# Fetching the last tile's rows of the last gather by single-row DMAs from SyncE and ScalarE instead of GpSimd

## The reference, cut to what matters

```python
x = x + 0.5 * ffn(layernorm(x))
x = x + attention(layernorm(x))
x = x + 0.5 * ffn(layernorm(x))

# ffn: t = rmsnorm(x) * scale; 32 experts, the best 4 for each token
vals, idx = top_k(t @ gate_w.T + gate_b, 4)
w = softmax(vals)
combine[token, idx] += w
h = swiglu(einsum('th,efh->tef', t, w1) + b1)          # for the chosen experts alone in the kernel
out = einsum('tef,ehf->th', h * combine, w2) + combine @ b2
result = t_in + out
```

## Time and profile before

| | |
|---|---|
| median of three runs | 724.93 us |
| the profiled execution's span | 722.9 us |
| TensorE busy | 531.0 us (73%) |
| GpSimd busy | 506.2 us (70%) |
| VectorE busy | 436.2 us (60%) |
| ScalarE busy | 347.2 us (48%) |
| GpSimd's 256 gathers (L564) | 245.0 us busy, 957 ns each |
| DMA, mean over the span | 150 GB/s |

### The profile page before, as it was taken

How to read it: one execution, slowest core, us unless ns; L and a number is a source line. 1 busy time by engine, 2 the same in 40 slices (tenths; PEclk the granted TensorE clock), 3 DMA queues, 4 the chain that set the end, 5 groups by cost and what they waited for, 6 DMA issues and landing times. The chain is left out here.

```text
span 722.9 us, 12843 instructions
## 1 busy us (share of the span) xinstructions
PE 531.0 (73%) x3252; PEld 443.8 (61%) x3253; DVE 436.2 (60%) x1243; ACT 347.2 (48%) x752; POOL 506.2 (70%) x551
## 2 busy tenths in 40 slices
PE   6258879999899999385607854999999999933000
PEld 3154366999899998253504553699998999833000
DVE  6889233555547778378993868255564767845222
ACT  4444413666556666495606644366665666610000
POOL 3677777777527777777677777777752777767765
PEclk9556999999999999797557955999999999977555
DMA  7997115566546664222111111456655666524222
GB/s 271 392 375 289 52 54 153 197 194 200 175 147 197 199 210 154 81 54 53 48 52 54 51 52 55 138 182 208 203 168 177 201 198 206 160 78 128 66 62 58
DMA packets 56493, 108.28 MB, mean 150 GB/s; under 512 B 12576, under 2 KB 19968, under 8 KB 56320
## 3 DMA queue, kind: packets, MB, share of 16 engines
q1 hardware_dynamic: 40064, 74.13, 30.7%
q0 software_dynamic: 16384, 33.59, 16.1%
HBM read 51.00 MB, written 56.62 MB: 149 GB/s over the span
## 5 line engine op out<-in xcount | busy, mean ns | idle before, releaser
L564 POOL DMA_INDIRECT YG<-ys,row x256 | 245.0, 957 | 116.9 <-issue 75.4
L539 POOL DMA_INDIRECT xs<-U,row x256 | 250.7, 979 | 81.9 <-issue 74.6
L1311 PE MATMUL PS<-W,xT 128*128 x768 | 182.2, 380 | 0.2
L1311 PEld LDWEIGHTS PS<-W,xT 128*128 128x128 f32 x768 | 138.4, 190 | 16.1 <-issue 1.2
L1005 DVE TENSOR_SCALAR glulin<-PS 128x512 f32<-128x512 f32 x96 | 66.3, 691 | 127.8 <-PE PS L1320 84.3
L626 ACT ACTIVATE yrow<-PS 128x512 f32<-128x512 f32 x96 | 57.3, 597 | 103.3 <-PE PS L1320 103.3
L1320 PEld LDWEIGHTS PS<-W,hidT 128*128 128x128 f32 x768 | 100.7, 193 | 7.8 <-issue 3.4
L1320 PE MATMUL PS<-W,hidT 128*128 x768 | 102.8, 277 | 1.6 <-issue 1.2
L1018 DVE SCALAR_TENSOR_TENSOR hid<-glulin,swish 128x512 f32<-128x512 f32 x96 | 66.6, 694 | 16.0 <-ACT swish L631 10.5
L631 ACT ACTIVATE swish<-glulin 128x512 f32<-128x512 f32 x96 | 60.4, 629 | 30.5 <-DVE glulin L1005 26.7
L639 ACT ACTIVATE xT<-PS 128x512 f32<-128x512 f32 x96 | 56.3, 589 | 38.8 <-PE PS L1214 38.7
(11 more groups left out here) (178 smaller groups left out, 714.2 us busy)
## 6 DMA issues: line engine op xcount, KB each, us to landing
xrow<-xs SPq DMA_DIRECT2D x96, 256.0 KB
ys<-yrow SPq DMA_DIRECT2D x96, 256.0 KB
xs<-YG SPq DMA_DIRECT2D x6, 2048.0 KB, 13.7
W<-in_w12T SPq DMA_DIRECT2D x1, 6144.0 KB, 33.5
xs<-U,row POOLq DMA_INDIRECT x256
YG<-ys,row POOLq DMA_INDIRECT x256, 2.5
out<-X SPq DMA_DIRECT2D x7, 256.0 KB, 2.6
X<-in_x SPq DMA_DIRECT2D x4, 256.0 KB, 3.6
```

The lines of the kernel that those rows point to most:

```text
L539: pool.indirect_dma_start(out=xs[c], out_offset=bass.IndirectOffsetOnAxis(ap=row[:, i:i + 1], axis=0), in_=U[:, (c * CT + t) * H:(c * CT + ...
L564: pool.indirect_dma_start(out=YG[:, t * TOPK + k, :], out_offset=None, in_=ys[c], in_offset=bass.IndirectOffsetOnAxis(ap=row[:, i:i + 1], ...
L1311: last = te.matmul(h1, xT[:, r, q * P:(q + 1) * P], W[:, bass.ds(es[q], 2 * H)], start=True, stop=True)
```

## The change

Tile 15 of phase 3 is left out of GpSimd's gather, which ends with tile 14. Its 128 rows x 4 choices are fetched by a new function, `gather_rows`: for each partition p the four slots are loaded from `row` into registers of the issuing engine, and four DMAs of one row (512 bytes) each are issued, with the register in their source address. SyncE fetches partitions 0 to 63, 32 of them ahead of the four stores of chunk 0 and 32 ahead of those of chunk 1; ScalarE fetches partitions 64 to 127 behind its last copies. Both wait first until all of yrow is stored and phase 2 is added (`combined` at 192), since tile 15's place in YG is still read until then.

On VectorE the last two tiles change places: tile 15 is added first, after `sync_gathered` and `act_gathered` have counted all 512 DMAs, and tile 14 last, its last addition behind `last_gathered`. SyncE's stores at the end are tiles 12 and 13, tile 15, and tile 14.

```diff
+SYNC_ROWS = 64
...
+        def gather_rows(eng, first, stop, done):
+
+            t, c = CT - 1, NCHUNK - 1
+            for p in range(first, stop):
+                i = c * PAIRS + t * TOPK
+                _, at = nc.values_load_multi_w_load_instructions(
+                    row[p:p + 1, i:i + TOPK], engines=[eng.engine], min_val=0, max_val=SLOTS - 1,
+                    skip_runtime_bounds_check_because="the ranks and the tiles' begins keep them below SLOTS")
+                for k in range(TOPK):
+                    eng.dma_start(YG[p:p + 1, t * TOPK + k, :], ys[c][bass.ds(at[k], 1), :]).then_inc(done, 16)
...
@@ sync
+            for r in range(2):
+                sp.wait_ge(yrow_stored[r], 16 * (NG // 2) * NPHASE)
+            sp.wait_ge(combined, PAIRS * (NPHASE - 2) + TOPK * CT)
             for c in range(NCHUNK):
+                gather_rows(sp, SYNC_ROWS // 2 * c, SYNC_ROWS // 2 * (c + 1), sync_gathered)
                 for g in range(NCG):
...
-                    n = CG - 1 if t + CG == NTILE else CG
+                    n = CG - 2 if t + CG == NTILE else CG
...
-            sp.wait_ge(combined, PAIRS * NPHASE)
-            sp.dma_start(out_v[NTILE // CG - 1][:, CG - 1], X[:, (NTILE - 1) * H:NTILE * H]).then_inc(out_stored, 16)
+            for n in (CG - 1, CG - 2):
+                if n == CG - 2:
+                    sp.wait_ge(combined, PAIRS * NPHASE)
+                t = NTILE - CG + n
+                sp.dma_start(out_v[NTILE // CG - 1][:, n], X[:, t * H:(t + 1) * H]).then_inc(out_stored, 16)
@@ gpsimd, gather(ph)
-                for t in range(CT):
+                last = CT - 2 if ph == NPHASE - 1 else CT - 1
+                for t in range(last + 1):
...
-                        ).then_inc(last_gathered if ph == NPHASE - 1 and (t, k) == (CT - 1, TOPK - 1)
+                        ).then_inc(last_gathered if ph == NPHASE - 1 and (t, k) == (last, TOPK - 1)
@@ scalar
             experts(1)
             add_b2(1)
+            for r in range(2):
+                act.wait_ge(yrow_stored[r], 16 * (NG // 2) * NPHASE)
+            act.wait_ge(combined, PAIRS * (NPHASE - 2) + TOPK * CT)
+            gather_rows(act, SYNC_ROWS, P, act_gathered)
@@ vector, combine(ph, first, stop)
-                    pairs[-1:] = [(stop - 2,), (stop - 1,)]
+                    pairs[-1:] = [(stop - 1,), (stop - 2,)]
...
+                    if ph == NPHASE - 1 and t0 == CT - 1:
+                        dve.wait_ge(sync_gathered, 16 * TOPK * SYNC_ROWS)
+                        dve.wait_ge(act_gathered, 16 * TOPK * (P - SYNC_ROWS))
+                    else:
+                        for t in tiles:
+                            dve.wait_ge(gathered[t % 2], 16 * (TOPK * ((ph * CT + t) // 2 + 1) - ending))
```

More of the change, by code:

```diff
@@ L267, in build @@
         last_gathered = sem("last_gathered")
+        sync_gathered = sem("sync_gathered")
+        act_gathered = sem("act_gathered")
         combined = sem("combined")
@@ L391, in _ @@
                     t = c * CT + g * CG
-                    n = CG - 1 if t + CG == NTILE else CG
+                    n = CG - 2 if t + CG == NTILE else CG
                     sp.dma_start(out_v[c * NCG + g][:, 0:n], X[:, t * H:(t + n) * H].rearrange("p (t h) -> p t h", h=H))\
                         .then_inc(out_stored, 16)
-            sp.wait_ge(combined, PAIRS * NPHASE)
-            sp.dma_start(out_v[NTILE // CG - 1][:, CG - 1], X[:, (NTILE - 1) * H:NTILE * H]).then_inc(out_stored, 16)
-            sp.wait_ge(out_stored, 16 * (NCHUNK * NCG + 1))
+            for n in (CG - 1, CG - 2):
[3 more added lines that the diff above has]
+                sp.dma_start(out_v[NTILE // CG - 1][:, n], X[:, t * H:(t + 1) * H]).then_inc(out_stored, 16)
+            sp.wait_ge(out_stored, 16 * (NCHUNK * NCG + 2))
         @block.gpsimd
@@ L1045, in combine @@
                 if ph == NPHASE - 1:
-                    pairs[-1:] = [(stop - 2,), (stop - 1,)]
+                    pairs[-1:] = [(stop - 1,), (stop - 2,)]
+                done = PAIRS * ph + TOPK * first
                 for tiles in pairs:
                     t0, n = tiles[0], len(tiles)
-                    ending = ph == NPHASE - 1 and t0 == CT - 1
-                    for t in tiles:
-                        dve.wait_ge(gathered[t % 2], 16 * (TOPK * ((ph * CT + t) // 2 + 1) - ending))
+                    ending = ph == NPHASE - 1 and t0 == CT - 2
+                    if ph == NPHASE - 1 and t0 == CT - 1:
[4 more added lines that the diff above has]
+                            dve.wait_ge(gathered[t % 2], 16 * (TOPK * ((ph * CT + t) // 2 + 1) - ending))
                     if t0 > first:
-                        dve.wait_ge(combined, PAIRS * ph + TOPK * (t0 - 2))
+                        dve.wait_ge(combined, done - TOPK * 2)
                     for k in range(TOPK):
@@ L1056, in combine @@
                             if k:
-                                dve.wait_ge(combined, PAIRS * ph + TOPK * t0 + n * (k - 1) + t - t0 + 1)
+                                dve.wait_ge(combined, done + n * (k - 1) + t - t0 + 1)
                             if ending and k == TOPK - 1:
@@ L1064, in combine @@
                                                    part if k else xt, ALU.mult, ALU.add).then_inc(combined, 1)
+                    done += TOPK * n
                     if ph < NCHUNK:
```

## The result

The kernel went from 724.85 us (4 runs) to 811.86 us (4 runs, 810.2 to 813.42), a ratio of 1.122 with a 95% interval of 1.120 to 1.124. The prediction was 816.5 us, in a range of 765 to 890. The profiled execution has a span of 810.9 us.

What follows compares the result with a forecast made beforehand. GpSimd's gather issue was taken as the bound. ScalarE's start at 650.1 plus 157.8 us of rows, the last landing at 809.4, 5.0 us of additions and store, and 2.0 from span to time gave 816.5 us, range 765 to 890.

Steps and rivals of the forecast that it cites:

- What bounds it and what goes: End of kernel: GpSimd's gather issue rate sets the end; removing tile 15's four gathers takes away 4 x 1.25 = 5.0 us.
- ScalarE last, VectorE behind it: ScalarE's rows end at 807.9, SyncE's at about 799; VectorE waits, then adds tiles 15 and 14, 1.53 us each.
- ScalarE's start: ScalarE's sequencer is free for its single rows at 650.1, when its closing DRAIN begins.
- The price of a row: Per partition on each issuing sequencer: 0.37 + 4 x 0.524 = 2.47 us, 157.8 us for 64 rows.
- The DMA: Issue of one single-row DMA: 0.338 us, taken from SyncE's xrow load; 0.524 with register operations and gaps.
- The load: Register load of a row's four slots: 0.332 us as on TensorE, 0.37 with one gap.
- Register operations: Before each row DMA: FUSED_REGOPS 0.046 and MOVE 0.029 us, with three gaps of 0.037.
- cheap rows: Rival: a row DMA issues in 0.2 us, time 781 or 760; chance 0.17 for 755 to 790, 0.06 for 727 to 755.
- Dear rows: Rival: row DMAs cost 0.786 us as b1's, time 884; chance 0.15 for 840 to 890, 0.04 above.
- Shared issue: Rival: SyncE and ScalarE can't issue at once, 15 us more, 831; inside the forecast's 0.52 for 790 to 840.
- The faster rival: Rival: a row DMA issues in a fraction of 128-partition ones; break-even 0.166 us with register operations; chance 0.04.

Runs made afterwards that it cites:

- The sizes: Changed kernel without tile 15's fetch; SyncE and ScalarE issue fixed-address DMAs of 1 to 128 rows, then register loads with single-row DMAs: 723.07 us beside 723.55.

## Why the prediction was right

*What bounds it and what goes.* Right. GpSimd's gathers set the end; four of them are 5.0 us by the prediction, and without them the end came 4.7 us (in the trace) or 4.9 us (by the ratio) earlier.

*ScalarE last, VectorE behind it.* Right, in the order forecast: SyncE's rows ended at 791 (799 expected), ScalarE's last DMA started at 804.7 (807.5), tile 15 and tile 14 took 805.95 to 808.92, 2.97 us (3.06), and 1.98 us followed to the end of the span (1.96).

*ScalarE's start.* 651.8 and not 650.1. Its last copy but one waited for TensorE until 651.74, where it began at 650.05. The stretch from 636.6 to 652 shows a granted clock of 0.50 (1.2 GHz) where the profile before had 0.69, a mean of both levels, and 16 turns took 3.67 us at 648.03 where they had taken 1.97 at 648.04. Why the clock differed there is not shown.

```profile
636.60:652.00 15.40, 7.62 (x35) 7.25 (x36) 7.19 (x12) 2.20 (x3) 11.57 (x13) 0.50 0.18 49
```

*The price of a row.* The sum, 2.47 us, was within 4% of the measured 2.39, and its main terms were off. Here is one row of SyncE in the chain of the changed kernel: start, us, what.

```profile
772.68 0.57 SPq L319
...
773.41 0.26 SPq L323
...
773.85 0.23 SPq L323
...
774.26 0.23 SPq L323
...
774.67 0.23 SPq L323
```

- The DMA: 0.214 to 0.225 us, not 0.338. I took the price of 128 rows, because the rows showed no fall from 128 partitions to 32. The sizes show why they couldn't: all of them lie on the flat part above 16 rows. Over four DMAs that is 0.45 to 0.5 us a row too much.
- The load: 0.57 to 0.60 us, not 0.332. TensorE's price doesn't hold for SyncE and ScalarE: 0.25 us a row too little.
- The first DMA behind a load on ScalarE: 0.467 instead of 0.271 in the run of the sizes. No row of before showed it: 0.2 us a row too little.
- Register operations: one FUSED_REGOPS and one MOVE for each DMA, 37 and 29 ns, with gaps of 0.03 to 0.04. Near the forecast (46, 29, 0.037).

- Outside the row: ScalarE started 1.7 us later than forecast, and the last row was there 1.2 us after its DMA's start and not 1.9.

So the closeness to 816.5 is in part luck: errors of 0.45 us a row in opposite directions, some 29 us each over 64 rows. The bounds of the issue time did not hold either. They were 0.441 to 0.786 us for a DMA with its register operations and gaps, and SyncE's DMAs in the lines above start 0.41 us apart. The range held because it reached down to the cheap rows, and because the load was dearer than forecast.

*The Trainium skill beside the row.* The Trainium skill, "DMA: Bandwidth & Descriptors", in its section on why a DMA increments its semaphore by 16, says that software can split a contiguous single row over 16 engines. This case's trace shows no such split: ScalarE's queue q10 carried 256 DMAs in 512 packets and 0.13 MB, one packet of 512 bytes and one more for each.

The same page of the Trainium skill, in "Issuing engines are not separate DMA queues", calls the time to initiate a DMA usually small relative to the DMA itself. For one row the trace agrees: 0.21 us of issue against 1.2 us to the landing. For many it is no measure of the cost, since landings overlap and the issues of one sequencer don't: 94 us of nothing but loads and issues. The 0.338 us that the prediction set against that sentence was the issue of a whole xrow load and not of 512 bytes.

*The rivals.* Cheap rows (760 to 781) had the right issue time, 0.2 us, and missed the load. Dear rows didn't occur. Shared issue is out: SyncE's rows start 2.26 us apart before ScalarE begins at 651.8 and 2.26 us apart beside it, and ScalarE's 2.34 us apart beside SyncE and after SyncE has ended its rows at 791 (the mean of 2.39 holds some rows of 2.6 to 2.9). The faster rival needed 0.166 us for a DMA with its register operations; the operations and gaps alone take 0.16 to 0.19, and the DMA 0.214.

## What to carry to other kernels

A single-row DMA cost its issuing sequencer more than half of what one of 128 rows did (0.25 and 0.43 us), so work that one indirect DMA of 1.25 us does for 128 rows is not taken over by 128 issues of 0.6 us each, a quarter of a register load included: count the issues, multiply by the smallest issue time in the trace, and compare with the idle stretch before anything else. The price of an operation on one engine's sequencer (a register load on TensorE) is an estimate for another's, and should widen the range. Before a piece is taken off the path, look whether it is hidden there: the last of four gathers saved nothing, four saved 4.7 to 4.9 us.

## What the runs showed of the hardware that I had not expected

- The issue time of a DMA on SyncE grows in steps from 0.252 us (1 and 2 rows of 512 bytes) over 0.30 (4 and 8) to 0.42 (16) and stays there (0.43 for 128).
- A register load of four values takes 0.57 us on SyncE and 0.60 on ScalarE, but 0.33 on TensorE; one value costs the same as four, two and eight 0.2 to 0.3 us more. ScalarE's next DMA is 0.2 us dearer.
- With single rows from consecutive addresses issued one in 0.15 us over both engines, the last was there 13.7 us after its issue instead of 1.2, and GpSimd waited up to 11.65 us for its own gathers. At one in 0.30 us, from scattered addresses, neither was seen.
- Beside a kernel before of 856 to 870 us, SyncE and ScalarE issued two to eleven DMAs in 10 us during GpSimd's last gathers, while GpSimd kept 1.25 us a gather, and about 17 to 34 in 10 us once it had ended. What slows them there is open.
